# Two 3x3 convolutions per layer: from four 128x32 tiles of the array to sixteen 32x32 tiles, a pair of images at a time

## The reference, cut to what matters

```python
for j in range(4):
    Kj = K[j] - K[j].mean(axis=(-2, -1), keepdims=True)    # 32 x 32 x 3 x 3
    z = conv3x3(x, Kj)                   # conv1
    z = relu(batchnorm(z, gamma[j], beta[j]))   # mean and variance over all images and pixels
    z = conv3x3(z, flip(transpose(Kj)))  # conv2
    x = batchnorm(x + 0.1 * z, gamma[j], beta[j])
    x = real(ifft2(fft2(x) / (1 + 0.1 * abs(fft2(Lj)) ** 2)))   # per channel
```

## Time and profile before

| | us |
|---|---|
| median of three launches | 718.09 (717.79 to 719.38) |
| profiled launch, its own time | 717.11 |
| its span, first to last instruction | 715.3 |
| TensorE busy, of the span | 653.2 (91%) |
| DVE busy | 518.6 (73%) |
| ACT busy | 264.1 (37%) |
| GpSimd busy (prologue alone) | 95.6 (13%) |
| mean granted TensorE clock | 0.973 |

### The profile page before, as it was taken

How to read it: one execution, slowest core, us unless ns; L and a number is a source line. 1 busy time by engine, 2 the same in 40 slices (tenths; PEclk the granted TensorE clock), 3 DMA queues, 4 the chain that set the end, 5 groups by cost and what they waited for, 6 DMA issues and landing times.

```text
span 715.3 us, 13262 instructions
## 1 busy us (share of the span) xinstructions
PE 653.2 (91%) x5408; PEld 223.5 (31%) x5408; DVE 518.6 (73%) x875; ACT 264.1 (37%) x416; POOL 95.6 (13%) x92
## 2 busy tenths in 40 slices
PE   7598999999998989998999899998998999989992
PEld 4222333323332433233333332233333322333330
DVE  2669877865997894639968945499788454997883
ACT  1455666652930031529200314291003243900033
POOL 0366666770000000000000000000000000000000
PEclk9699999999999999999999999999999999999996
DMA  9994111117500022772000227720003187000034
GB/s 183 182 167 83 32 32 31 31 31 172 139 1 1 1 59 62 167 155 78 1 1 1 63 58 175 149 76 1 1 1 94 29 198 156 6 1 1 1 99 137
DMA packets 44637, 51.05 MB, mean 71 GB/s; under 512 B 36385, under 2 KB 36514, under 8 KB 42530
## 3 DMA queue, kind: packets, MB, share of 16 engines
q1 hardware_dynamic: 40098, 48.92, 31.8%
q10 hardware_dynamic: 4480, 1.30, 1.1%
HBM read 11.92 MB, written 4.19 MB: 23 GB/s over the span
## 4 chain that ended last, share of the span: by engine, by line
PE 61%; DVE 27%; ACT 6%; issue 3%; DMA 1%; SPq 1%; POOL 0%; DVEq 0%; ACTq 0%; POOLq 0%
PE psum L939 32%; PE psum L1013 7%; PE psum L1109 5%; PE psum L1076 4%; DVE stats L830 3%; DVE X L827 3%; DVE work L839 3%; PE psum L1092 3%; DVE tabT L821 3%; PE psum L1123 3%; DVE work L849 3%; DVE work L883 2%; PE psum L962 2%; ACT Z L567 2%; PE psum L1001 2%
## 5 line engine op out<-in xcount | busy, mean ns | idle before, releaser
L939 PE MATMUL psum<-Z,wts 128*32 128x512 f32 x1536 | 168.9, 595 | 6.3 <-DVE Z L809 6.3
L939 PE MATMUL psum<-X,wts 128*32 128x512 f32 x1536 | 170.0, 593 | 0.1
L741 DVE BATCH_NORM_STATS2 stats<-Z 128x6 f32<-128x512 f32 x60 | 41.3, 692 | 78.8 <-ACT Z L504 78.7
L939 PEld LDWEIGHTS psum<-Z,wts 128*32 128x32 f32 x1536 | 51.5, 109 | 123.8 <-issue 109.7
L939 PEld LDWEIGHTS psum<-X,wts 128*32 128x32 f32 x1536 | 48.0, 109 | 111.1 <-issue 110.1
L567 ACT ACTIVATE Z<-Z,small 128x512 f32<-128x512 f32 (+4 forms) x92 | 79.9, 922 | 5.2 <-DVE small L799 4.7
L504 ACT ACTIVATE Z<-psum 128x512 f32<-128x512 f32 x64 | 38.1, 595 | 106.2 <-PE psum L939 94.9
L582 ACT ACTIVATE work<-psum 128x64 f32<-128x64 f32 x16 | 4.5, 281 | 197.0 <-PE psum L1100 197.0
L1109 PE MATMUL psum<-work,cstS 128*128 128x512 f32 x128 | 59.2, 605 | 4.7 <-DVE work L849 3.9
L827 DVE SCALAR_TENSOR_TENSOR X<-psum,X 128x512 f32<-128x512 f32 x64 | 43.2, 675 | 18.2 <-PE psum L939 18.1
L1092 PE MATMUL psum<-work,cstS 128*128 128x496 f32 x128 | 56.3, 582 | 0.0
(11 more groups left out here) (114 smaller groups left out, 777.1 us busy)
## 6 DMA issues: line engine op xcount, KB each, us to landing
X<-X SPq DMA_DIRECT2D x64, 260.0 KB, 4.0
Z<-Z SPq DMA_DIRECT2D x32, 520.0 KB, 8.1
Z<-x SPq DMA_DIRECT2D x36, 128.0 KB, 4.2
out<-Z SPq DMA_DIRECT2D x24, 128.0 KB, 2.3
parS<-par SPq DMA_DIRECT2D x4, 673.0 KB, 8.4
Z<-x SPq DMA_DIRECT2D x12, 120.0 KB, 5.3
Z<-x ACTq DMA_DIRECT2D x14, 64.0 KB, 4.3
Z<-x SPq DMA_DIRECT2D x14, 64.0 KB, 5.0
```

The costliest lines, as they stand in the source:

```text
L741: nc.vector.bn_stats(stats[:, 6 * c:6 * c + 6], rows(Z0, REG, c // Q, CH * (c % Q), CH))
L939: last = nc.tensor.matmul(out_b[C * r:C * r + C, :], weights[:, o:o + C], rows(src, reg, bp, g, CH, dj - 1), start=(dj == 0), stop=(dj == ...
```

## The change

Each matmul becomes one of K = 32 input channels and M = 32 output channels on a tile of 32x32. All four chunks of a pair are computed together in four banks, in nine steps t. A tap of the kernel is a row shift di and a column shift dj; `conv_plan` gives each chunk k, at each step, the block distance `rel` and the tap, so that at any step the four chunks use different row blocks of the array, and the four residues c different column blocks: 16 matmuls on 16 tiles. Where a chunk goes from one row block to the next (steps 3, 5 and 7, `SWITCHES`), TensorE waits for its own matmuls of the step before on that bank. All four banks are claimed before the first step, both halves of the copy must have landed, and the banks are signalled full in the last step. The copy (now X1, Z1) is shifted by one row, in DMAs of 32 and of 96 partitions.

```diff
+GROUPS_BEHIND = (BEHIND, BEHIND + Q)
+SWITCHES = (3, 5, 7)
+def conv_plan(k):
+    plan, used = [], {-1: 0, 0: 0, 1: 0}
+    for i in range(R):
+        rel = (k + i) % R
+        for di in TAP_OF_ROWS[rel][k]:
+            plan.append((rel, di, used[di]))
+            used[di] += 1
+    return plan
...
 def prologue_chunk(c):
-    if c >= BEHIND:
-        order.append(("conv1", 0, c - BEHIND))
+    if c in GROUPS_BEHIND:
+        order += quarters("conv1", 0, GROUPS_BEHIND.index(c))
...
-    return order + [("sum", NCH - 1)] + [("conv1", 0, c) for c in range(NCH - BEHIND, NCH)]
+    return order + [("sum", NCH - 1)] + quarters("conv1", 0, 2) + quarters("conv1", 0, 3)
...
 def layer_steps(j):
-        5: fourier(j, 0, "fwdW"),
-        9: fourier(j, 0, "fwdH") + fourier(j, 1, "fwdW"),
-        13: fourier(j, 0, "invH") + fourier(j, 1, "fwdH") + fourier(j, 2, "fwdW"),
-        15: fourier(j, 1, "invH") + fourier(j, 2, "fwdH"),
+        1: fourier(j, 0, "fwdW"),
+        2: fourier(j, 0, "fwdH") + fourier(j, 1, "fwdW"),
+        3: fourier(j, 0, "invH") + fourier(j, 1, "fwdH") + fourier(j, 2, "fwdW") + fourier(j, 1, "invH") + fourier(j, 2, "fwdH"),
     }
-    for c in range(NCH):
-        steps += [("conv2", j, c), ("turn", j, c)] + after.get(c, [])
+    for bp in range(BP):
+        steps += quarters("conv2", j, bp) + after.get(bp, [])
...
-    rest = {1: fourier(j, 3, "invH"), 3: fourier(j, 2, "invW"), 5: fourier(j, 3, "invW")}
-    for c in range(NCH):
+    rest = {0: fourier(j, 3, "invH") + fourier(j, 2, "invW"), 1: fourier(j, 3, "invW")}
+    for bp in range(BP):
         if j + 1 < DEPTH:
-            steps.append(("conv1", j + 1, c))
-        steps += rest.get(c, [])
+            steps += quarters("conv1", j + 1, bp)
+        steps += rest.get(bp, [])
...
-        turned = (squares[:, 0:2 * N], squares[:, 2 * N:4 * N], third[:, :])
+        turned = (squares[:, 0:2 * N], squares[:, 2 * N:4 * N], third[:, :], rest[:, 2 * N:4 * N])
...
-            eng.dma_start(dst[0:2 * C, d + GROUP:d + GROUP + n], src[2 * C:128, s:s + n]).then_inc(done, 16)
-            eng.dma_start(dst[2 * C:128, d:d + n], src[0:2 * C, s:s + n]).then_inc(done, 16)
+            eng.dma_start(dst[0:C, d + GROUP:d + GROUP + n], src[3 * C:128, s:s + n]).then_inc(done, 16)
+            eng.dma_start(dst[C:128, d:d + n], src[0:3 * C, s:s + n]).then_inc(done, 16)
...
+            def relu_pair(j, bp):
+                act.wait_ge(z1_in[bp], 32 * (j + 1))
+                parts = [(Z0, REG, G)]
                 if bp:
+                    parts.append((Z1, REG2, G + 1))
+                for t, reg, n in parts:
+                    z = rows(t, reg, bp, 0, n)
+                    last = nc.scalar.activation(z, z, ACT.Relu, bias=small[:, 13:14], scale=small[:, 12:13])
                 last.then_inc(relu_done, 1)
...
+            STATS_LAST = (*range(2 * Q, NCH - Q), NCH - 2, NCH - 1, NCH - 4, NCH - 3)
+
             def conv1_stats(j, c):
                 n = NUMBER["conv1", j, c]
-                if c == NCH - 1:
+                if c >= NCH - 2:
                     bk.full(n)
                     nc.vector.bn_stats(stats[:, 6 * c:6 * c + 6], bank(n)).then_inc(last_stats, 1)
...
             def relu_first(j):
-                for g, n in ((1, CH), (1 + CH, CH), (1 + 2 * CH, G - 1 - 2 * CH)):
-                    z = rows(Z2, REG2, 0, g, n)
+                z = rows(Z1, REG2, 0, 0, G + 1)
...
                         if at[1] == NCH - 1:
                             link(ins)
                             aggregate()
-                    elif what == "turn":
                         if at[1] % 2:
                             turn(at[1])
...
+            def conv(before, first, bp, X, copy, weights):
+                for k in range(Q):
+                    bk.claim(first + k)
+                for t in range(TAPS):
+                    for k in range(Q):
+                        if t in SWITCHES:
+                            pe.wait_ge(rows_switched, len(SWITCHES) * Q * before + Q * SWITCHES.index(t) + k + 1)
+                        for c in range(R):
+                            p, copied, di, dj, g, skip, n = conv_step(k, t, c)
+                            o = C * (3 * di + 3 + dj)
+                            src, reg = (copy, REG2) if copied else (X, REG)
+                            last = nc.tensor.matmul(bank(first + k)[C * c:C * c + C, ROW * skip:ROW * (skip + n)],
+                                                    weights[C * p:C * p + C, o:o + C],
+                                                    rows(src, reg, bp, g, n, dj - 1, C * p, C * p + C),
+                                                    start=(t == 0), stop=(t == TAPS - 1), tile_position=(C * p, C * c))
+                        if t + 1 in SWITCHES:
+                            last.then_inc(rows_switched, 1)
+                        if t == TAPS - 1:
+                            last.then_inc(filled[(first + k) % BANKS], 1)
+
+            def conv1(j, bp):
...
+                for h in range(2):
+                    pe.wait_ge(x1_in[bp][h], 32 * (j + 1))
```

190 lines of the change are left out of this document (82 added, 108 removed).

## The result

The changed kernel takes **875.06 us** (869.55 to 880.48, four launches), against 717.94 us for the kernel before in the same session: ratio 1.2185, 95% interval 1.2106 to 1.2263. The profiled launch took 875.31 us, its span 873.4 at a mean granted clock of 0.889. That mean gives about 194 us of the span at 1.2 GHz (0.111 x 2 x 873.4), against 39 before (0.027 x 2 x 715.3).

A forecast was written before the change was run, and what follows sets the result against it. VectorE was taken to bound the conv2 stage, TensorE conv1 and the prologue. Starts 4 x 2.1, conv2 4 x 12.8, conv1 3 x 3.5, prologue 2 and clock 16 made 88 on 717.1: 805, median 806 us, range 755 to 850.

The forecast's parts named there:

- a pair on the array: Convolutions: 18 passes at 0.43 us plus 0.8 for three switches; array free after 8.5 us, against 10.5 before.
- start of conv2: Ahead of each conv2 stage: relu_first as one piece starts conv2 later, +2.1 us a layer.
- prologue: Before the layers: +6.1 us behind the last sum, -4 (0 to -9) before it, together +2.
- clock: Whole launch: new TensorE idles each bring a fall to the lower clock, +16 us (0 to +25).
- the conv2 stages: VectorE gets each pair late and idles; a stage ends at 83.3 us against 70.5, +12.8 a layer.
- the conv1 stages: Later copies and statistics outweigh 8 us saved by four pairs instead of 16 chunks: +3.5, three times.
- The bounds, 7.7 and 17.8: Time of a pair on sixteen tiles: 7.7 us without switch loss, 17.8 at 62 ns for each of 288 records.
- The rule that I set aside: Weight loads overlap matmuls only in another row group: about 0.11 us more a pass, a pair 10.5; judged contradicted.
- The order of the waits: In the stages: VectorE idles 4.6 and 6.3 us in conv2; prepare_taps ahead of move_back delays conv1's last pair.
- only because it waits for banks: Conv2 stage before the change: TensorE merely looks busy, while VectorE works 61.7 of its 70.6 us.
- The rival of sixteen tiles that are not fed: Convolutions: 62 ns a record, 17.8 us a pair, launch about 1040 us; chance 5%.
- The faster rival: TensorE's array bounds every stage, launch about 654 us; test: conv2's third pair starts within 20 us; chance 7%.

The follow-up runs named there:

- b3: The kernel before with BEHIND 16 instead of 5, so no chunk of the first convolution lies inside the prologue; 750.85 us.
- b5: b2 with the old prologue, one chunk of the first convolution behind each sum again; 739.58 us, ratio 1.0308.
- b2: The changed kernel's order and claims by pair on the old four 128x32 tiles, each chunk signalled when done; 771.97 us, ratio 1.0761.
- e1: The changed kernel with each chunk kept on one row block for all steps and the waits between row blocks dropped; 858.71 us.
- e4: The changed kernel with prepare_taps moved behind c8's statistics, so behind the last pair's move_back; 866.67 us, ratio 1.2001.
- e11: The changed kernel with the shifted copies of z cut to an eighth of their bytes; 873.63 us.
- e9: The changed kernel with unused matmuls keeping TensorE busy in its three long waits of each layer; 865.48 us, ratio 1.2059.
- e6: e1 with every convolution matmul streaming a quarter of its columns (128); 797.1 us.
- b1: The changed kernel's order, claims and signal at the pair's end, on the old four 128x32 tiles; 883.28 us, ratio 1.2282.

## Why the prediction was wrong in size and right in sign

| step | forecast | measured (layer 0 or 1) |
|---|---|---|
| a pair on the array | 8.5 us | 9.92 |
| DVE's first addition after conv2's start | 8.8 | 9.85 |
| fwdW of pair 0 | 28.1 | 29.1 |
| third pair starts | 31.1 | 32.6 |
| DVE idle before pairs 3 and 4 | 4.6 / 6.3 | 6.24 / 7.21 |
| fwdW of pair 1 | 49.5 | 52.3 |
| fourth pair starts, ends | 51.6, 60.4 | 55.9, 66.2 |
| second pair of conv1, from the last fwdW of conv2's stage | 32.4 | 32.6 |
| last pair of conv1 starts, ends | 57.5, 66.3 | 59.1, 73.6 |
| start of conv2 | +2.1 a layer | +3.1 |
| prologue | +2 | +32.3 |
| clock | +16 | about +17 (estimate) |

Against the sum, the prologue missed by 30 us, the conv2 stages by 18 (81.5 against 51.2 and their 12 of clock), the conv1 stages by 17 (32 against 10.5 and 4.5 of clock), the starts by 4: 69 in all, the whole difference between 806 and 875.

**The prologue** is the step that failed outright. "12.7 less for TensorE; ... I take -4 (0 to -9)" counted the single chunks as time to be saved. They had been free. "The prologue is TensorE's too (20.00 of 20)" was read rightly off, but it did not follow that less work would end sooner: b3, with eleven chunks less, reached the last sum no sooner, for TensorE then waited for the other engines. I had even written that DVE idles in the blocks, and then priced the blocks at less than nothing. Each of the two is added whole: the two chunks that hold them are 9.5 and 9.7 us longer than before. The rest of the 23.7 us ahead of the last sum I read as the lower clock (some records of `sum` take 1.06 us instead of 0.62), which no run tested. b5 against b2 puts 28.7 us on the placement.

**The pair** was mis-sized, at 8.5 instead of 9.92. "As passes on more tiles have kept their pitch" carried the 0.43 us of eight tiles over to sixteen. They keep it for the first two steps (0.44); without waits the mean is 0.54. The three waits, priced at 0.8, lengthen their steps by 1.5 us, and removing them saves 0.28. The bounds, 7.7 and 17.8, held. Three pair times lie on the path of a conv2 stage: 4 x 3 x 1.4 = 17 of its 18 us. The rule that I set aside (the Trainium skill, TensorE: Matmul & The Clock Gate, Part 3: Packing small matmuls: loads overlap matmuls only if they go to another row group) gave, as an estimate, 0.11 us more a pass. By that number e1 agrees in the mean, with 0.106 (0.536 - 0.43). In its mechanism the trace does not bear the rule out: in e1's first two passes all 32 loads start within 0.14 us, so the second pass's loads go out while the first pass runs on the same tiles, and both passes keep 0.43; the old kernel's four loads a pass did overlap too. Whether the loads are what slows the later steps, no run here shows.

**The order of the waits** was right: which bank is claimed, where DVE idles, where TensorE does, that `prepare_taps` delays the last copy (e4). Every start in the table lies within 4.3 us of its forecast, and they drift apart by the length of a pair. One reading under it was wrong: in the conv2 stage before, TensorE did not look busy "only because it waits for banks"; its matmul starts there leave 3.9 of 70.6 us beyond the pitch, so it was as full as DVE, and the forecast did not need the claim. In the conv1 stage the last pair failed: I let it start 1.6 us too early and run 8.8 us. It takes 14 to 15: its first two steps at 1.2 GHz (1.7 us), the holes (2.3 to 3.7 us by e11), and the longer passes. "The DMAs carry the same bytes" overlooked that the instructions are bytes too, 1.49 MB in place of 0.70, and that TensorE stands still when they are late. That +16 for the clock and e9's 17 agree confirms nothing: e9's number has a margin of about its own size.

The rival of sixteen tiles that are not fed, 62 ns a record, is excluded by 9.92 us for 288 records (34 ns), and by e6's shorter steps. The faster rival is excluded by its own test, the third pair 32.6 us into the stage and not within 20.

What the change costs, part by part: 718 before; 740 with relu, statistics, claims and conv2's order by pair (b5); 772 with the prologue's blocks (b2); 883 with the signal at the end of a pair (b1); 875 with sixteen tiles instead of four. So the sign was not luck: the hand-over outweighs the array by far. No kernel here beats the one before. Even with the grain for free, 0.43 us a pair on 32 pairs are 14 us at most.

## What to carry to other kernels

When a change makes the unit of work larger, price the hand-over before the arithmetic: the engine behind it starts one unit later at every stage, and whatever is queued behind its wait goes with it. Here that cost 111 us, against about 8 gained on the array. A filler step that costs nothing when it is cut small can be added whole when it is four times as long, and a TensorE that is busy for 20 of 20 us need not be what sets the pace: with less to do it waited for the others. To see whether work is hidden, take it out once and look whether anything behind it moves.
